# Low-rank attention: row products as two 64-row products side by side, shifts moved by DMA, items in one bank

## The reference, cut to what matters

```
c_q  = h @ W_DQ + b_DQ                  # 32 features
c_kv = h @ W_DKV + b_DKV                # 32 features
q_c, k_c, v_c = c_q @ W_UQ, c_kv @ W_UK, c_kv @ W_UV     # 8 heads of 128
q_r, k_r = c_q @ W_QR, h @ W_KR         # 32 features for a head; k_r shared by heads
scores = (q_c . k_c + q_r . k_r) / sqrt(160)
out = softmax(scores) @ v_c, heads joined, @ W_O + b_O
```

## Time and profile before

| | us |
|---|---|
| median of 3 runs (2118.95 to 2120.53) | 2120.36 |
| profiled execution, its own time | 2113.35 |
| its span | 2111.6 |
| PE busy | 1900.0 (90%) |
| DVE busy | 1529.3 (72%) |
| ACT busy | 1312.7 (62%) |
| POOL busy | 1207.2 (57%) |

### The profile page before, as it was taken

One profiled execution on the slowest core, in us unless ns is written; L12 is line 12 of the kernel. 1 busy time (PEld: TensorE's weight loads), 2 busy tenths in 40 slices (PEclk: granted clock), 3 DMA queues, 4 the chain that ended last, 5 costly groups with the idle time before them and its releaser, 6 DMA issues.

```text
span 2111.6 us, 42114 instructions
## 1 busy us (share of the span) xinstructions
PE 1900.0 (90%) x15727; PEld 1369.4 (65%) x15727; DVE 1529.3 (72%) x3304; ACT 1312.7 (62%) x2965; POOL 1207.2 (57%) x1135
## 2 busy tenths in 40 slices
PE   4769898989855989999999999999999999999949
PEld 4657777777744746666666666666666666666636
DVE  4668888888856677777777776776776786777554
ACT  4657877777734437566566666665665675666624
POOL 4100000000024528888788788787788788888865
PEclk8889999999966769999999999999999999999966
DMA  3636545655200000000000000000000000000002
GB/s 97 150 91 153 137 132 141 151 129 142 62 23 1 1 0 6 9 9 6 9 9 6 9 9 6 9 9 6 9 9 6 9 9 6 9 9 9 9 7 79
DMA packets 125518, 88.70 MB, mean 42 GB/s; under 512 B 75607, under 2 KB 100482, under 8 KB 125186
## 3 DMA queue, kind: packets, MB, share of 16 engines
q1 hardware_dynamic: 125314, 86.01, 16.3%
HBM read 39.83 MB, written 37.75 MB: 37 GB/s over the span
## 4 chain that ended last, share of the span: by engine, by line
PE 64%; DVE 20%; ACT 9%; issue 4%; POOL 2%; DMA 1%; SPq 0%; ACTq 0%; DVEq 0%; POOLq 0%
PE pair L1504 11%; PE pair L1412 11%; PE pair L1463 8%; PE pair L1459 8%; DVE amax L1420 6%; ACT prob L978 5%; DVE o_inv L1522 4%; ACT y L504 3%; PE pair L1511 3%; PE pair L1213 2%; PE pair L900 2%; DVE mx_neg L1021 2%; PE pair L1207 2%; PE pair L790 2%; PE pair L1280 1%
## 5 line engine op out<-in xcount | busy, mean ns | idle before, releaser
L1474 ACT ACTIVATE prob<-pair 128x512 f32<-128x512 f32 x1024 | 597.9, 598 | 443.1 <-PE pair L1463 399.3
L1420 DVE TENSOR_REDUCE amax<-pair 128x1 f32<-128x512 f32 x1024 | 664.2, 675 | 123.4 <-PE pair L1412 121.1
L1412 PE MATMUL pair<-key_hl,q_hi 128*128 128x512 f32 x1024 | 455.1, 447 | 27.5 <-DVE amax L1420 17.5
L1463 PE MATMUL pair<-q_low,key_h 66*128 66x512 f32 x1024 | 405.4, 396 | 0.0
L1459 PE MATMUL pair<-q_hi,key_hl 128*128 128x512 f32 x1024 | 404.0, 395 | 0.0
L1488 POOL TENSOR_TENSOR Wm<-Wm,prob 128x1024 f32<-128x1024 f32 x160 | 381.4, 2384 | 36.1 <-ACT prob L1474 24.0
L1488 POOL TENSOR_TENSOR w_mix<-w_mix,prob 128x1024 f32<-128x1024 f32 x160 | 381.6, 2385 | 16.4 <-ACT prob L1474 3.1
L978 ACT ACTIVATE prob<-pair,mx_neg 128x128 f32<-128x128 f32 x1024 | 294.3, 388 | 116.3 <-DVE mx_neg L1021 109.0
L485 POOL TENSOR_SCALAR veps<-mv 128x8 f32<-128x8 f32 x48 | 11.5, 240 | 587.9 <-DVE mv L455 586.6
L1412 PEld LDWEIGHTS pair<-key_hl,q_hi 128*128 128x128 f32 x1024 | 195.7, 191 | 171.3 <-DVE amax L1420 74.9
L1504 PE MATMUL pair<-prob,values 128*32 128x256 f32 x4096 | 250.3, 385 | 0.0
(11 more groups left out here) (186 smaller groups left out, 2637.0 us busy)
## 6 DMA issues: line engine op xcount, KB each, us to landing
rows_mem<-once SPq DMA_DIRECT2D x256, 128.0 KB, 2.6
queries<-rows_mem SPq DMA_DIRECT2D x64, 256.0 KB, 4.9
keys<-rows_mem SPq DMA_DIRECT2D x16, 1024.0 KB, 5.4
yT<-o_norm SPq DMA_DIRECT2D x256, 32.0 KB, 1.8
x<-x_dram SPq DMA_DIRECT2D x8, 512.0 KB, 7.3
out_dram<-x SPq DMA_DIRECT2D x8, 512.0 KB, 3.2
Wm<-w_mla_dram SPq DMA_DIRECT2D x1, 1168.0 KB, 5.5
Wt<-w_dram SPq DMA_DIRECT2D x1, 501.0 KB
```

Of the source, the lines that this page charges most:

```text
L1412: e.matmul(bank(ROW_BANKS[i]), q_hi[:, k, t * P:(t + 1) * P], key_hl[:, b % 2, i * HALF:(i + 1) * HALF], start=True, stop=True, skip_group ...
L1420: e.tensor_reduce(amax1[:, u % 2, t, i:i + 1], bank(ROW_BANKS[i]), AX_X, ALU.max).then_inc(*row_maxed.up((r, i)))
L1463: e.matmul(bank(j), key_h1[:, b % 2, ks], q_low[:, k, sl], start=False, stop=True, skip_group_check=True).then_inc(*key_scored.up((g, half)))
L1474: e.activation(prob1[:, g % P_BUFS, half * HALF:(half + 1) * HALF], bank(K_BANKS[(2 * g + half) % 3]), ACT.Exp, scale=SCALE1).then_inc(*ke ...
```

## The change

The row-score product of 128 contracted rows for each half of the keys becomes a pair of products of 64 rows: the first half of the keys against partitions 0 to 63, the second half against partitions 64 to 127. For this the key's rounded part is also written to partitions 64 to 127 of a new tile `key_h2`. Each product of the pair writes its own bank, and three banks (4, 5, 6) are used in turn. Both wait for one maximum, that of the first half of the tile before. The pair is issued ahead of the four key-score products of its step. A tile of queries is now every fourth one of 512 (`every_fourth`), so its weights are read at a step of four elements. The remainder of the key no longer enters the row scores.

The shift becomes one part, written by GpSimd in two operations into four adjacent columns, and SyncE moves them by one DMA for each half of a head (128 pieces of four elements) to row 64 of `q_low`. The transposes on TensorE and the copies on ScalarE are gone. The accumulating key product has 65 rows. All items of the stage's steps use bank 7; batch items start at even g that have no query. The lead of the row scores is 12 steps, that of the plan 14; the reciprocals come one step later after the second weighing.

```diff
-ROW_LEAD = 13
-PIPELINE = 15
+ROW_LEAD = 12
+PIPELINE = 14
...
-    had, banks = {}, itertools.cycle((6, 7))
-    def begin(item):
-        j = next(banks)
+    had, opening_banks = {}, itertools.cycle((4, 5, 6, 7))
+    def begin(item, j=7):
...
-        for kind, i, at in (("query", 0, -15), ("query", 1, -11), ("shift", 0, -6), ("shift", 1, -2)):
-            u, rest = divmod(g - at, NT)
+        for i in range(2):
+            u, rest = divmod(g + 14 - 4 * i, NT)
...
-        if item is None and waiting and (g % NT in (0, 3, 4) or g >= NT * U):
+        if item is None and waiting and (g % 2 == 0 or g >= NT * U):
...
-            run = begin(item)
+            run = begin(item, 6 if item == ("proj", B - 1, 1) else 7)
...
+        key_h2 = sb("key_h2", [P, 2, HALF], F32R, low)
...
-        K_BANKS, PVB, ROW_BANKS, MISC = (0, 1, 2), 3, (4, 5), 6
+        K_BANKS, PVB, ROW_BANKS, MISC = (0, 1, 2), 3, (4, 5, 6), 6
...
-            elif kind == "shift":
-                e.wait_ge(*shift_steps.at((a, i, 4)))
-                for t in range(4):
-                    ins = e.matmul(bank(j)[0:KR + 2, t * P:(t + 1) * P], shift_cols[:, i, t, :], eye_r[:, :],
-                                   start=True, stop=True, skip_group_check=True)
...
-            elif kind == "shift" and part == 2:
-                e.wait_ge(*shift_turned.at((a, i)))
-                queries_free(e, a)
-                e.activation(q_low[KR:KR + 2, a % Q_BUFS, sl], bank(j)[KR:KR + 2, :], ACT.Copy).then_inc(
...
                 e.activation(key_h1[0:KR, a % 2, sl], bank(j)[0:KR, :], ACT.Identity, bias=b_keys[0:KR])
+                if i == 1:
+                    e.activation(key_h2[KR:P, a % 2, :], bank(j)[KR:P, :], ACT.Identity, bias=b_keys[KR:P])
...
-        def pe_row_scores(e, r, i):
+        def every_fourth(queries, t):
+            return queries.rearrange("k (i q t) -> k i t q", i=2, t=4)[:, t // 4, t % 4, :]
+
+        def pe_row_scores(e, r):
...
-            if r:
-                e.wait_ge(*row_maxed.at((r - 1, i)))
-            e.matmul(bank(ROW_BANKS[i]), q_hi[:, k, t * P:(t + 1) * P], key_hl[:, b % 2, i * HALF:(i + 1) * HALF],
-                     start=True, stop=True, skip_group_check=True).then_inc(*row_scored.up((r, i)))
+            if r == 0:
+                e.wait_ge(*const_ready.at(0))
+                e.wait_ge(*value_ready.at(0))
+            else:
+                e.wait_ge(*row_maxed.at((r - 1, 0)))
+            halves = key_h1[0:KR, b % 2, 0:HALF], key_h2[KR:P, b % 2, :]
+            for i, rows in enumerate((slice(0, KR), slice(KR, P))):
+                e.matmul(bank(ROW_BANKS[(2 * r + i) % 3]), every_fourth(q_hi[rows, k, :], t), halves[i],
+                         start=True, stop=True, skip_group_check=True).then_inc(*row_scored.up((r, i)))
...
-            e.tensor_tensor(sk, c, mc, ALU.subtract).then_inc(*shift_steps.up((u, i, 2)))
+            if u:
+                e.wait_ge(*shift_ready(u - 1, i))
+            e.tensor_tensor(shift_cols[:, i, :], c, mc, ALU.subtract).then_inc(*shift_steps.up((u, i, 2)))
+
+        def sync_move_shift(e, u, i):
             e.wait_ge(*shift_steps.at((u, i, 2)))
-            e.tensor_copy(shift_cols[:, i, :, KR], sk).then_inc(*shift_steps.up((u, i, 3)))
-            e.wait_ge(*shift_steps.at((u, i, 3)))
-            e.tensor_tensor(shift_cols[:, i, :, KR + 1], sk, shift_cols[:, i, :, KR], ALU.subtract).then_inc(
-                *shift_steps.up((u, i, 4)))
+            queries_free(e, u)
+            e.dma_start(q_low[KR:KR + 1, u % Q_BUFS, i * HALF:(i + 1) * HALF].bitcast(F32).rearrange(
+                "o (p t) -> o p t", t=4), shift_cols[:, i, :].bitcast(F32)).then_inc(shift_moved[u % Q_BUFS][i], 16)
...
-                for half in range(2):
-                    if 0 <= g + ROW_LEAD < total:
-                        pe_row_scores(e, g + ROW_LEAD, half)
-                    if 0 <= g < total:
+                if 0 <= g + ROW_LEAD < total:
+                    pe_row_scores(e, g + ROW_LEAD)
+                if 0 <= g < total:
+                    for half in range(2):
                         pe_key_scores(e, g, half)
...
-                u, t = divmod(g - 12, NT)
+                u, t = divmod(g - 13, NT)
                 if t == 0 and 0 <= u < B * NH:
                     dve_invert_totals(e, u, 0)
...
-            for u in range(B * NH):
-                sync_move_head(e, u)
+            for u in range(B * NH + 2):
+                if u < B * NH:
+                    for i in range(2):
+                        sync_move_shift(e, u, i)
+                if u >= 2:
+                    sync_move_head(e, u - 2)
```

More of the change, by code:

```diff
@@ L202, in low_rank_plan @@
     U = B * NH
-    PARTS = {"query": 3, "shift": 2, "turn": 2, "cq": 3, "key": 3, "const": 2, "value": 2, "proj": 2}
-    had, banks = {}, itertools.cycle((6, 7))
-    def begin(item):
-        j = next(banks)
+    PARTS = {"query": 3, "turn": 2, "cq": 3, "key": 3, "const": 2, "value": 2, "proj": 2}
+    had, opening_banks = {}, itertools.cycle((4, 5, 6, 7))
+    def begin(item, j=7):
         before = had.get(j)
@@ L216, in regular @@
     def regular(g):
-        for kind, i, at in (("query", 0, -15), ("query", 1, -11), ("shift", 0, -6), ("shift", 1, -2)):
-            u, rest = divmod(g - at, NT)
+        for i in range(2):
+            u, rest = divmod(g + 14 - 4 * i, NT)
             if rest == 0 and 0 <= u < U:
-                return kind, u, i
+                return "query", u, i
         return None
@@ L227, in low_rank_plan @@
             continue
-        run = begin(item)
+        run = begin(item, next(opening_banks))
         for part in range(1, PARTS[item[0]] + 1):
@@ L380, in build_program @@
         low = ExitStack()
-        eye_r = sb("eye_r", [P, P], F32R, low)
         w_high = sb("w_high", [QR + 2, NH, KR + 1], F32R, low)
@@ L389, in build_program @@
         key_hl = sb("key_hl", [P, 2, T], F32R, low)
-        key_h1 = sb("key_h1", [KR + 2, 2, T], F32R, low)
+        key_h1 = sb("key_h1", [KR + 1, 2, T], F32R, low)
+        key_h2 = sb("key_h2", [P, 2, HALF], F32R, low)
         values = sb("values", [P, 2, NT, DC], F32, low)
@@ L394, in build_program @@
         q_hi = sb("q_hi", [P, Q_BUFS, T], F32R, low)
-        q_low = sb("q_low", [KR + 2, Q_BUFS, T], F32R, low)
+        q_low = sb("q_low", [KR + 1, Q_BUFS, T], F32R, low)
         amax1 = sb("amax", [P, 2, NT, 2], F32, low)
-        shift = sb("shift", [P, 2, 3, 4], F32, low)
-        shift_cols = sb("shift_cols", [P, 2, 4, KR + 2], F32R, low)
+        shift = sb("shift", [P, 2, 2, 4], F32, low)
+        shift_cols = sb("shift_cols", [P, 2, 4], F32R, low)
         prob1 = sb("prob1", [P, P_BUFS, 1024], F32, low)
@@ L1228, in build_program, with shift_ready @@
         row_scored, row_maxed, row_topped = signal("row_scores"), signal("row_half_maxima"), signal("row_maxima")
-        shift_steps, shift_turned, shift_ready = signal("shift_steps"), signal("shift_turned"), signal("shift_rows")
+        shift_steps = signal("shift_steps")
+        shift_moved = [(new_sem(f"shift_row_{k}_first_half"), new_sem(f"shift_row_{k}_last_half")) for k in range(Q_BUFS)]
+        def shift_ready(u, i):
+            return shift_moved[u % Q_BUFS][i], 16 * (u // Q_BUFS + 1)
         key_scored, key_exp, pv_done = signal("key_scores"), signal("key_exponentials"), signal("weighed_values")
@@ L1268, in pe_low_part @@
                          skip_group_check=True).then_inc(*query_done.up((a, i)))
-            elif kind == "shift":
-                e.wait_ge(*shift_steps.at((a, i, 4)))
-                for t in range(4):
-                    ins = e.matmul(bank(j)[0:KR + 2, t * P:(t + 1) * P], shift_cols[:, i, t, :], eye_r[:, :],
-                                   start=True, stop=True, skip_group_check=True)
-                ins.then_inc(*shift_turned.up((a, i)))
             elif kind == "proj":
+                if a == B - 1 and i == 1:
+                    e.wait_ge(*row_maxed.at((total - 1, 1)))
                 for moved in o_moved:
@@ L1297, in pe_low_part @@
                 for t in range(NT):
-                    ins = e.matmul(bank(j)[:, t * NH:(t + 1) * NH], cq[:, a % 2, t * P:(t + 1) * P], w_const[:, :],
+                    ins = e.matmul(bank(j)[:, t * NH:(t + 1) * NH], every_fourth(cq[:, a % 2, :], t), w_const[:, :],
                                    start=True, stop=True, skip_group_check=True)
@@ L1419, in dve_row_max @@
                 e.wait_ge(*row_topped.at((u - 2, t // 4)))
-            e.tensor_reduce(amax1[:, u % 2, t, i:i + 1], bank(ROW_BANKS[i]), AX_X, ALU.max).then_inc(
+            e.tensor_reduce(amax1[:, u % 2, t, i:i + 1], bank(ROW_BANKS[(2 * r + i) % 3]), AX_X, ALU.max).then_inc(
                 *row_maxed.up((r, i)))
@@ L1433, in pool_shift @@
             ts4 = slice(4 * i, 4 * i + 4)
-            top, mc, sk = (shift[:, i, n, :] for n in range(3))
+            top, mc = (shift[:, i, n, :] for n in range(2))
             c = ccol[:, b % 2, ts4, h]
```

(2 more changed lines are left out.)

14 lines of the change are left out of this document (3 added, 11 removed).

## The result

| | before | changed |
|---|---|---|
| median, us | 2119.68 | 2211.62 (2210.0 to 2214.24) |
| profiled execution, us | 2113.35 | 2212.91 |

The ratio is 1.0435 with a 95% interval of 1.0417 to 1.0453: 92 us slower, where I had forecast 2105 and a range up to 2150. The sign and the size were wrong.

What follows compares the result with a forecast made beforehand. TensorE was taken to bound the low-rank stage, with VectorE setting the pace after the second weighing. Heads -5, batch items -7, opening and end -3 took 2113.35 to 2098, or 2105 as median; range 2045 to 2150.

Steps and rivals of the forecast that it cites:

- the new step's sum: Low-rank stage on TensorE: pair 0.235, changes of division 0.34, four key products of 0.235; 1.51 us against 1.41.
- the slow rival: Pair's strided weight loads take 0.107 us longer each two, unhidden: step 1.62, head 18.4 to 18.5, 2146 us; chance 0.22.
- Two changes of division: TensorE switching between 64-row pair and 128-row products, into and out of each pair: 0.34 us together per step.
- The clock: TensorE's granted clock, 1.00 in the low-rank stage before; falling below 1.00 there was named as a sign of being wrong.
- Batch items: Batch work in the low-rank stage, nearly all exposed: 13.5 us a batch put at 12.5, -7 us over seven batches.
- Opening and end: One row step less to fill, one step less in all, and a shorter GpSimd tail: -3 us together.
- half-fast rival: Half the change of division paid around pairs: step 1.34 us, total 2047; fast or half fast together had chance 0.20.
- The pair takes the time of one product: TensorE's two 64-row products overlap, taking 0.235 us in the stream instead of 0.47 serially.
- the worked head: A low-rank-stage head without batch items, followed step by step on TensorE and VectorE: 17.82 us against 17.90 before.
- The fast rival: No change of division paid around the pairs; steps follow VectorE at 1.19 us, total 2014; fast or half fast 0.20.
- the serial one: The pair's two products on TensorE don't overlap: step 1.75 us, about +90 us, total 2200; chance 0.05.
- bank waits: Bank 7's items queue ahead of TensorE's rows, or the shift comes late: 2130 to 2150 us; chance 0.08 for both.

Runs made afterwards that it cites:

- same-row run: The adjacent run with both products of the pair on partitions 0 to 63, so they cannot lie side by side; 2267.39 us, ratio 1.0732.
- full-row run: The adjacent run with each row product at its full 128 rows instead of a pair of 64 rows; 2089.64 us, ratio 0.9886.
- adjacent run: The changed kernel with adjacent weights for pair and const item, and four one-column shift DMAs per half of a head; 2133.04 us, ratio 1.0101.
- pair-alone run: The kernel before with only the 64-row pair ahead of the key products, adjacent weights, two banks, waiting for the second maximum; 2242.40 us, ratio 1.0615.

## Why the prediction was wrong

**The step that failed: the new step's sum, 0.235 + 0.34 + 4 x 0.235 = 1.51, which left the pair's weight load at the price of adjacent weights.** The step measured 1.67 to 1.70 and the head 18.66 instead of 17.82, 54 us over 64 heads. I had the load at a stride of four elements as the slow rival with 0.22, by which nothing hides a load behind a change of division, where every pair stands. That was the case: 0.306 against 0.183 with adjacent weights, 0.12 where the rival had 0.107. It should have been the forecast, or nearly, and was not because no row showed a strided load and I took the contiguous rows as nearest.

**A term that was too small.** Two changes of division: 0.34 taken, and 0.39 measured with adjacent weights (0.43 + 0.43 - 2 x 0.235). How much of it is the change and how much the load that stands still was not taken apart. The step was 1.57 against 1.51. The rival's step with both errors is 1.70, not 1.62, and its head 18.66, not 18.4 to 18.5.

**A term that was missing, and nearly as large.** The clock: 0.95 instead of 1.00 between 1000 and 2000 us, some 41 us by the intervals above. I named its fall as what would make me wrong and gave it neither a chance nor a price, though the kernel before has such a fall twice, at 846 and 1470, both right behind the value item. The const item's strided weights (0.85 a batch) were missing as well: I had counted only the row tiles.

**The smaller terms.** Batch items, put at 12.5 us a batch, take 14.2 in the batch with one fall (167.5 - 3.9 - 8 x 18.67), the const item's 0.85 among them: 12 us over seven batches. Opening and end, put at -3, came to +2.6: the first reciprocal starts 9.5 us later, with the clock at 0.50 up to 798 where the kernel before had 1.00 from 786 on, and the end is 6.9 shorter. For the profiled execution the forecast was 2098 and 2212.91 was measured, 115 apart; 54 + 41 + 12 + 6 is 113 of them, an estimate. In the half-fast rival I had taken 16 us off for items and opening where the other rivals have 10; with 10 it is 2053, still in the range.

**The loss by runs.** By ratios, each with its part of the clock: stride 1.033 (70 us), side by side instead of full rows 1.022 (45), all else 0.989 (-24). Together that is 91 of the 92; since each ratio is taken against the one before, they add up by construction.

**What held.** The pair takes the time of one product (rows of the window stage; the same-row run). With adjacent weights the worked head came out: behind the second weighing the fourth pair starts after 5.21 us (5.27 in the working) and the first weighing ends at 8.71 (8.74). The rest has four steps at 1.57 instead of 1.51, and the head was 17.90 to 17.95 against 17.82. With the strided load the reciprocals hardly show in the chain any more, so TensorE sets the pace almost alone. The full-row head, 17.66 expected, was 17.5. DMA, bank and GpSimd cost nothing that shows. The fast rival fell by the 0.2 of each change, the serial one by the same-row run, bank waits by the full-row run.

Left open: why the clock falls in the fourth interval of every batch of the changed kernel and of the adjacent run, but only twice in the stage of the kernel before and in few batches with full rows, and why it holds 0.99 in the pair-alone run, which is slower still. The cost of the falls is measured; their cause is not shown.

## What to carry to other kernels

Here two changes of division per pair (0.39 us) cost more than the one product saved (0.235). So group the divided products or leave them whole; grouping was not tried here. Between 1200 and 1800 us of the changed kernel the load behind such a change stood still every time: so look at its stride first, and count every load that the new layout touches. Give the clock a price in the sum if the trace before has even one fall. When one engine's burst stalls another through double buffers, a third buffer can be worth most when each product waits for its own: that and the interleaving it allows, tried only together, gave 52 us here, more than anything in the change.

## What the hardware showed that I had not expected

A load of 128 weight columns of 4 bytes takes 0.183 to 0.191 us at a step of 4 or 8 bytes and 0.306 to 0.312 at 16; at 4 and at 16 bytes 64 and 128 rows hardly differ. In a stream of 512-column products even the slow one adds at most 0.01 for two. The granted clock can fall to its lower level right behind 2.5 us of light products while TensorE shows as fully busy, and one such fall costs 1.6 us in the kernel before and 3.9 with pairs.
